# A decoder layer on one core: turned halves stored in two transfers instead of four, one load, eight weight casts and two additions moved

## The chip, the cores and the metric

The kernel runs on one core of a Trainium2 chip. The metric is the device time of one execution in microseconds (us). A core has a matrix engine (TensorE, PE in the rows; PEld are its weight loads), a vector engine (VectorE, DVE), an activation engine (ScalarE, ACT), a general engine (GpSimd, POOL) and a queue engine that issues transfers (SyncE, SP; SPq in the rows), besides 16 DMA engines that move the data. Each of the five runs its own list of instructions in order; they meet at semaphores, which count up when an instruction or a transfer is done.

## The reference, cut to what matters

```python
x = x + attn(layernorm(x))             # x: 2 x 512 x 1024, float32
x = x + fake_quant(layernorm(x)) @ fake_quant(ctx)   # ctx: 2 x 1024 x 1024
x = x + experts(layernorm(x))          # 64 experts of rank 8, top 16

def attn(h):                           # 32 query heads, 8 key/value heads of 128
    q, k, v = h @ Wq, h @ Wk, h @ Wv   # Wq 1024 x 4096, Wk and Wv 1024 x 1024
    q, k = rope(q), rope(k)            # second half of a head turned into the first
    p = softmax(causal(q @ k.T / sqrt(128)))
    return (p @ v) @ Wo                # Wo 4096 x 1024
```

Only the attention block is touched by the change.

## The kernel before, in words

Products in float32 are made of three passes: each factor is split into a high part (a rounded copy, type fp32r, by a cast) and a low part (factor minus high part), and hi·hi, hi·lo and lo·hi are summed in PSUM (`PASSES`). So each operand of PE costs one cast and one subtraction on other engines before PE can use it. The large products are made by a seven-product scheme of Winograd's kind (`P1` to `P7`) on quarters of the matrices.

After a first stage (four panels of Wq, Wk, Wv; some 160 us) the program runs 64 **units** `u`. A unit is one query head for one of the two batch rows. PE's list for a unit is: scores(u), one place of filling work, mix(u-1) (probabilities times values), a second place of filling work, and the transposes of the unit's probabilities (`turn_probs`, L1733), in three chunks. What fills:

- In units 1 to 56 it is **jobs**: 112 of them, `JOB_AT` says which at which unit and place. Seven jobs (`SEQ`: P1, P6, P2, P7, P5, P4, P3) make one **narrow panel** `e` of 16, that is two heads of q or k for both batch rows. VectorE reads each product (`read_job`); for P2/P4 (batch row 0) and P5/P3 (batch row 1) it multiplies with sine and cosine (L1293, L1294), GpSimd adds (`turn_added`) and SyncE stores the result to HBM (`keep_turned`, L556 to L563), once after P4 and once after P3. The tiles that hold the two **turned halves** `made_half(b, i)` lie in SBUF on 128 partitions: partitions 0 to 63 belong to head n = 0, partitions 64 to 127 to head n = 1; i = 0 holds the first half of the head's channels for n = 0 but the second for n = 1, and i = 1 the reverse. Each of the four pieces of 64 rows of 2 KB is one transfer of 128 KB. They count `q_kept[b]` up by 16 each, 64 for a panel and batch row.
- Three things wait for `q_kept`: VectorE before it overwrites the tiles for the next panel (P2 waits for row 0, L1326; P7 for row 1, L1322), SyncE before it loads a q or k of that panel (`load_q` L541, `load_kv` L531), and ScalarE once (`first_high`, f = 1, L1024).
- From unit 57 on it is **first steps** `f` = 0 to 15, two in a unit (`STEP_AT`): products of the heads' outputs with Wo. Step f needs a cast and a low part of `first_rows(f)` (ScalarE L1027, GpSimd L852) and a cast and a low part of a pair of weight rows w00, 128 x 1024 (`ob_hi`: ScalarE L1029; `ob_lo`: VectorE L1395, in `first_weight_low`). The rows are loaded by SyncE in `load_first(f)`, L600.

In units with an even number up to 56 VectorE also adds a block of PSUM to the previous unit's output (`add_pair`, L1387 to L1389), for which the second chunk of the transposes waits. In units 50, 52, 55 and 56 (`SHORT`) there is one job instead of two; in 50 and 52 (`HALVED`) PE runs half of that job, then mix, then the other half. After the units follow 48 larger steps of the output product and then the other two blocks, which the change doesn't touch.

Of the kernel before, what the change touches and what calls it, by code (L numbers as in the profile page):

```python
# [282 lines left out]
def attention(nc, held, es, x_t, Wq, Wk, Wv, Wo, cos_in, sin_in, quant_in, ctx_rows, qk_dram, v_dram, o_dram,  # L283
# [219 lines left out]
    def _(sp):  # L503
# [22 lines left out]
        def load_kv(h):  # L526
            g, b = h // 2, h % 2
            if h >= 1:
                sp.wait_ge(kv_lo, 2 * h)
            if g >= HPG:  # L530
                sp.wait_ge(q_kept[b], 64 * (panel_of("k", g) + 1))  # L531
            sp.dma_start(kv_raw[:, 0, :], qk_dram[g, b]).then_inc(kv_in, 16)
            sp.dma_start(kv_raw[:, 1, :].rearrange("p (j c) -> p j c", c=HEAD),
                         v_dram[b * H:(b + 1) * H, g * HEAD:(g + 1) * HEAD].rearrange("(j p) c -> p j c", p=P)
                         ).then_inc(kv_in, 16)

        def load_q(u):
            if u >= 2:
                sp.wait_ge(q_lo, u - 1)
            if u >= 8:  # L540
                sp.wait_ge(q_kept[batch_of(u)], 64 * (panel_of("q", 4 * (u // 8) + u % 4) + 1))  # L541
            sp.dma_start(q_raw[:, u % 2, :], qk_dram[GROUPS + 4 * (u // 8) + u % 4, batch_of(u)]
                         ).then_inc(q_in[u % 2], 16)

        def load_narrow(e):
# [3 lines left out]
            for k in range(2):  # L549
                sp.dma_start(nraw[:, e % 2, k].rearrange("p k a c -> p k (a c)"),  # L550
                             W[k * 512:k * 512 + 512, head * HEAD:(head + 2) * HEAD].rearrange("(k p) c -> p k c", p=P)
                             ).then_inc(n_in[e % 2][k], 16)

        def keep_turned(j):
            if SEQ[j % 7] not in TURNS:
# [3 lines left out]
            sp.wait_ge(turn_made, 2 * e + b + 1)  # L559
            for n, (x, y) in enumerate(((0, 1), (1, 0))):  # L560
                rows = slice(64 * n, 64 * n + 64)
                sp.dma_start(qk_dram[head + n, b, 64 * x:64 * x + 64], made_half(b, 0)[rows, :]).then_inc(q_kept[b], 16)
                sp.dma_start(qk_dram[head + n, b, 64 * y:64 * y + 64], made_half(b, 1)[rows, :]).then_inc(q_kept[b], 16)  # L563

# [101 lines left out]
        for u in range(1, UNITS):  # L666
# [4 lines left out]
            if u == LAST_JOB_UNIT:  # L671
                load_first(0)
            if (u - 1, 0) in JOB_AT:
                keep_turned(JOB_AT[u - 1, 0])
# [9 lines left out]
            if u == LAST_JOB_UNIT:  # L684
                for f in range(1, 4):
                    load_first(f)
            if 2 <= u <= LAST_JOB_UNIT + 1:
# [254 lines left out]
    def _(act):  # L942
# [75 lines left out]
        def first_high(f):  # L1018
# [4 lines left out]
            if f == 1:  # L1023
                act.wait_ge(q_kept[0], 64 * NARROW)  # L1024
            if f >= 2:
                act.wait_ge(first_done, f - 1)
            nc.scalar.copy(oa[0][:, f % 2, :, 0:256], first_rows(f)).then_inc(fa_hi, 1)  # L1027
            act.wait_ge(w00_in[q // 4], 64)
            nc.scalar.copy(ob[0][:, f % 2, :, :], w00[:, 2 * q:2 * q + 2, :]).then_inc(fb_hi, 1)  # L1029

# [154 lines left out]
    def _(dve):  # L1185
# [126 lines left out]
        def read_job(j, begun=False):  # L1312
# [7 lines left out]
            elif p == "P7":  # L1320
                if e:
                    dve.wait_ge(q_kept[1], 64 * e)  # L1322
                nc.vector.tensor_tensor(n_u[:, 1, :], b, n_p1[:], ALU.add).then_inc(job_read, 1)
            elif p == "P2":
                if e:
                    dve.wait_ge(q_kept[0], 64 * e)  # L1326
                job_turned(b, made_half(0, 1), made_half(0, 0))
# [64 lines left out]
        def first_weight_low(f):  # L1392
            q = f % PAIRS
            dve.wait_ge(fb_hi, f + 1)
            nc.vector.tensor_tensor(ob[1][:, f % 2, :, :], w00[:, 2 * q:2 * q + 2, :], as32(ob[0][:, f % 2, :, :]),  # L1395
# [157 lines left out]
        for u in range(UNITS):  # L1553
# [12 lines left out]
            if u in SHORT:  # L1566
                normalise(u)
            if (u - 1, 2) in JOB_AT:
                read_job(JOB_AT[u - 1, 2])
            elif (u - 1, 1) in JOB_AT:  # L1570
                read_job(JOB_AT[u - 1, 1], read_begun(u))
            if (u, 1) in STEP_AT and u != LAST_JOB_UNIT + 3:
# [3 lines left out]
            if u == LAST_JOB_UNIT:  # L1576
                begin_last(JOBS - 1)
            if 0 < u <= PAIRED and u % 2 == 0:
                add_pair(u - 1)
# [964 lines left out]
```

## Time and profile before

| what | value |
|---|---|
| median of 3 runs | 1269.94 us (1269.48 to 1271.03) |
| the profiled execution | 1270.15 us, its span 1268.4 us |
| PE busy | 1247.6 us, 98% of the span |
| VectorE, ScalarE, GpSimd busy | 851.1, 788.0 and 612.4 us |
| DMA engines busy, units 1 to 56 | 0.67 of the time of 16 |
| TensorE clock granted | full speed all the time |

All times in the rows are us from the start of the span; the 1.75 us between span and execution lie around it. PE idles for some 20 us in all. A wait of another engine matters only where PE waits behind it. "Share" of DMA is the mean over the 16 DMA engines; the view doesn't tell one of them from another.

### The profile page before, as it was taken

The page shows a single profiled execution, that of the slowest core. Times are in us where ns is not written, and L with a number is a line of the kernel's source. Part 1 is how long each engine was busy: PE and PEld are TensorE (multiplying, and loading weights), DVE is VectorE, ACT ScalarE, POOL GpSimd, SP SyncE. Part 2 cuts the span into 40 slices and gives each one's busy share as a digit, 9 for nine tenths or more (in the row PEclk, how much of TensorE's full clock was granted, in tenths as well). Part 3 has the DMA queues.
Part 4 walks back from the last instruction along what each step waited for, and adds up shares of the span by engine and source line. Part 5 has one row for each costly group of instructions (what it writes and reads, how often), then busy time and mean ns, then how long its engine had stood idle before and what let it go on. Part 6 is the DMA issues. An engine that isn't in the chain of part 4 may idle for free. (4 is left out here: it accounts for less than half of the span.)

```text
span 1268.4 us, 19734 instructions
## 1 busy us (share of the span) xinstructions
PE 1247.6 (98%) x6823; PEld 1073.4 (85%) x6831; DVE 851.1 (67%) x1919; ACT 788.0 (62%) x1601; POOL 612.4 (48%) x450
## 2 busy tenths in 40 slices
PE   9999999999999999999999999999999999999998
PEld 8898898888888888888888887878888888868787
DVE  7874735566666667666666666655786777988863
ACT  6412247677768777778777888873333367766530
POOL 4776766678767877778677756420000000021100
PEclk9999999999999999999999999999999999999999
DMA  8043154454857958649586588658864567401111
GB/s 282 18 137 130 59 158 157 146 172 134 245 154 205 243 175 233 175 109 232 151 225 183 113 249 287 211 171 260 295 191 127 164 212 256 147 3 34 50 43 50
DMA packets 122403, 208.72 MB, mean 165 GB/s; under 512 B 15409, under 2 KB 56369, under 8 KB 118721
## 3 DMA queue, kind: packets, MB, share of 16 engines
q1 hardware_dynamic: 118272, 178.10, 43.0%
q0 software_dynamic: 4032, 29.36, 12.2%
q8 instruction: 55, 0.90, 0.3%
q14 instruction: 44, 0.35, 0.1%
HBM read 147.40 MB, written 88.08 MB: 186 GB/s over the span
## 5 line engine op out<-in xcount | busy, mean ns | idle before, releaser
L1359 DVE TENSOR_TENSOR pT_lo<-banks,pT_hi 128x512 fp32r<-128x512 f32 (+1 forms) x192 | 103.6, 595 | 114.3 <-ACT pT_hi L1059 114.2
L1811 PE MATMUL banks<-ob_hi,oa_hi 128*128 128x512 f32 x384 | 149.4, 389 | 0.0
L1811 PE MATMUL banks<-ob_lo,oa_hi 128*128 128x512 f32 x384 | 149.4, 389 | 0.0
L1811 PE MATMUL banks<-ob_hi,oa_lo 128*128 128x512 f32 x384 | 149.4, 389 | 0.0
L1768 PE MATMUL banks<-xc,nring_hi_a 128*128 128x512 f32 x448 | 138.6, 390 | 0.7 <-DVE q_made L1294 0.3
L1768 PE MATMUL banks<-xc,nring_hi_b 128*128 128x512 f32 x448 | 138.6, 391 | 0.0
L1043 ACT CAST oa_hi<-oraw 128x1024 fp32r<-128x1024 f32 x48 | 50.4, 1050 | 127.0 <-PE banks L1811 114.8
L2031 POOL TENSOR_TENSOR resid<-resid,colterm 128x1024 f32<-128x1024 f32 x8 | 19.9, 2491 | 205.1 <-ACT colterm L2089 132.6
L1059 ACT CAST pT_hi<-banks 128x512 fp32r<-128x512 f32 (+1 forms) x192 | 86.6, 527 | 45.2 <-PE banks L1733 44.5
L1716 PE MATMUL banks<-kT,q_hi 128*128 128x512 f32 (+2 forms) x384 | 104.1, 352 | 0.0
L786 POOL TENSOR_TENSOR q_lo<-q_raw,q_hi 128x512 fp32r<-128x512 f32 x64 | 88.7, 1386 | 27.0 <-ACT q_hi L997 27.0
L1370 DVE CUSTOM_DVE_ANT_0 prob<-banks,mask 128x512 f32<-128x512 f32 (+2 forms) x192 | 101.1, 551 | 0.3 <-DVE resid L1265 0.3
L1406 DVE TENSOR_TENSOR oa_lo<-oraw,oa_hi 128x1024 fp32r<-128x1024 f32 x48 | 58.8, 1225 | 61.4 <-ACT oa_hi L1043 61.2
L1768 PEld LDWEIGHTS banks<-xc,nring_hi_a 128*128 128x128 f32 x448 | 80.4, 188 | 14.9 <-issue 1.7
L1768 PEld LDWEIGHTS banks<-xc,nring_hi_b 128*128 128x128 f32 x448 | 80.7, 188 | 13.7
L1066 ACT ACTIVATE banks<-prob,small 128x384 f32<-128x384 f32 (+2 forms) x192 | 89.3, 465 | 0.0
L791 POOL TENSOR_TENSOR nring_lo_a<-nraw,nring_hi_a 128x512 fp32r<-128x512 f32 x48 | 63.4, 1321 | 51.2 <-ACT nring_hi_a L1011 51.1
L1768 PE MATMUL banks<-xc,nring_lo_a 128*128 128x512 f32 x224 | 87.3, 390 | 0.0
L1768 PE MATMUL banks<-xc,nring_lo_b 128*128 128x512 f32 x224 | 87.3, 390 | 0.0
L1811 PEld LDWEIGHTS banks<-ob_hi,oa_hi 128*128 128x128 f32 x384 | 72.1, 188 | 15.1
L1811 PEld LDWEIGHTS banks<-ob_lo,oa_hi 128*128 128x128 f32 x384 | 72.1, 188 | 15.0
L1811 PEld LDWEIGHTS banks<-ob_hi,oa_lo 128*128 128x128 f32 x384 | 72.1, 188 | 14.8
(275 smaller groups left out, 3415.8 us busy)
## 6 DMA issues: line engine op xcount, KB each, us to landing
q_raw<-qk_dram SPq DMA_DIRECT2D x64, 256.0 KB, 3.8
o_S<-o_st SPq DMA_DIRECT2D x64, 256.0 KB, 3.1
w<-in_L_attn_Wo SPq DMA_DIRECT2D x32, 512.0 KB, 6.7
oraw<-o_S SPq DMA_DIRECT2D x32, 512.0 KB, 4.0
nraw<-in_L_attn_Wq SPq DMA_DIRECT2D x28, 512.0 KB, 6.0
o_S<-o_S POOLq DMA_DIRECT2D x12, 1024.0 KB, 10.1
o_S<-o_N POOLq DMA_DIRECT2D x12, 1024.0 KB, 10.7
resid<-in_x SPq DMA_DIRECT2D x16, 512.0 KB, 7.3
```

The lines of the kernel that those rows point to most:

```text
L786: nc.gpsimd.tensor_tensor(qh[1][:, u % 2, :], q_raw[:, u % 2, :], as32(qh[0][:, u % 2, :]), ALU.subtract).then_inc(q_lo, 1)
L791: nc.gpsimd.tensor_tensor(split(n_ring(1, j)), n_factor(j), split(as32(n_ring(0, j))), ALU.subtract).then_inc(n_lo, 1)
L1043: nc.scalar.copy(oa[0][:, s % 2, :, :], oraw[:, s % 2, :, :]).then_inc(oa_hi, 1)
L1059: nc.scalar.copy(pT[0][:, chunk_at(u, c):chunk_at(u, c) + CHUNK_WIDTH[c]], turned_chunk(turned, mixed, c)).then_inc(pT_hi, 1)
L1066: nc.scalar.activation(prob[:, sl] if n == 0 else score_tile(i), prob[:, sl], ACT.Exp, bias=shift[:, i:i + 1], scale=-1.0, accum_out=total ...
L1359: nc.vector.tensor_tensor(pT[1][:, sl], turned_chunk(turned, mixed, c), as32(pT[0][:, sl]), ALU.subtract).then_inc(pT_lo, 1)
L1370: nc.vector.tensor_tensor_reduce(out=prob[:, PROB_AT[i]:PROB_AT[i] + w], in0=score[:, s, c:c + w], in1=mask[:, H - w:H] if i else first_ma ...
L1406: nc.vector.tensor_tensor(oa[1][:, s % 2, :, :], oraw[:, s % 2, :, :], as32(oa[0][:, s % 2, :, :]), ALU.subtract).then_inc(oa_lo, 1)
L1716: ins = nc.tensor.matmul(score[:, s, c:c + w], qh[a][:, u % 2, i * P:(i + 1) * P], kT[e][:, h % 2, 0:w], start=(p == 0), stop=(p == 2))
L1768: ins = nc.tensor.matmul(job_bank(j), n_ring(a, j)[:, k * P:(k + 1) * P], xc[:, XI[p], c, k, :], start=(opens and k == 0 and n == 0), stop ...
L1811: ins = nc.tensor.matmul(step_bank(m, t), oa[a][:, s % 2, k, t * P:(t + 1) * P], ob[c][:, s % 2, k, :], start=(q == 0 and k == 0 and i == ...
L2031: nc.gpsimd.tensor_tensor(resid[:, t, :], resid[:, t, :], colterm[:, t // TPB, :], ALU.add).then_inc(col_added, 1)
```

## The change

1. `keep_turned` stores each SBUF tile of 128 partitions in one transfer of 256 KB. The target in HBM is then a list of two pieces of 64 rows that are five (or three) pieces apart. `q_kept` counts to 32 for a panel and batch row instead of 64, and the four places that wait for it follow.
2. In unit 56 SyncE issues `load_first(1)` together with `load_first(0)`, ahead of the stores of that unit, and no longer behind them.
3. For even first steps (f = 0, 2, ..., 14) VectorE makes the cast of the weight pair itself, right ahead of its subtraction; ScalarE makes it for odd f only.
4. In units 50 and 52 VectorE's `add_pair` comes before `read_job`; in unit 52 the first addition of that job (`begin_last`) is taken ahead of it.

```diff
-                sp.wait_ge(q_kept[b], 64 * (panel_of("k", g) + 1))
+                sp.wait_ge(q_kept[b], 32 * (panel_of("k", g) + 1))
...
+        qk_halves = qk_dram.rearrange("h b (x r) c -> (h b x) r c", r=64)
+
         def keep_turned(j):
...
-            for n, (x, y) in enumerate(((0, 1), (1, 0))):
-                rows = slice(64 * n, 64 * n + 64)
-                sp.dma_start(qk_dram[head + n, b, 64 * x:64 * x + 64], made_half(b, 0)[rows, :]).then_inc(q_kept[b], 16)
-                sp.dma_start(qk_dram[head + n, b, 64 * y:64 * y + 64], made_half(b, 1)[rows, :]).then_inc(q_kept[b], 16)
+            first = 4 * head + 2 * b
+            for i, halves in enumerate((slice(first, first + 6, 5), slice(first + 1, first + 5, 3))):
+                sp.dma_start(qk_halves[halves], made_half(b, i)).then_inc(q_kept[b], 16)
...
             if u == LAST_JOB_UNIT:
                 load_first(0)
+                load_first(1)
...
             if u == LAST_JOB_UNIT:
-                for f in range(1, 4):
-                    load_first(f)
+                load_first(2)
+                load_first(3)
...
             nc.scalar.copy(oa[0][:, f % 2, :, 0:256], first_rows(f)).then_inc(fa_hi, 1)
-            act.wait_ge(w00_in[q // 4], 64)
-            nc.scalar.copy(ob[0][:, f % 2, :, :], w00[:, 2 * q:2 * q + 2, :]).then_inc(fb_hi, 1)
+            if f % 2:
+                act.wait_ge(w00_in[q // 4], 64)
+                nc.scalar.copy(ob[0][:, f % 2, :, :], w00[:, 2 * q:2 * q + 2, :]).then_inc(fb_hi, 1)
...
         def first_weight_low(f):
             q = f % PAIRS
-            dve.wait_ge(fb_hi, f + 1)
+            if f % 2:
+                dve.wait_ge(fb_hi, f // 2 + 1)
+            else:
+                if f:
+                    dve.wait_ge(first_done, f - 1)
+                else:
+                    dve.wait_ge(job_done, JOBS)
+                dve.wait_ge(w00_in[q // 4], 64)
+                link(nc.vector.tensor_copy(ob[0][:, f % 2, :, :], w00[:, 2 * q:2 * q + 2, :]))
...
+            third = u in HALVED and SEQ[JOB_AT[u - 1, 1] % 7] == "P3"
+            if third:
+                begin_last(JOB_AT[u - 1, 1])
+            if u in HALVED:
+                add_pair(u - 1)
...
-                read_job(JOB_AT[u - 1, 1], read_begun(u))
+                read_job(JOB_AT[u - 1, 1], read_begun(u) or third)
...
-            if 0 < u <= PAIRED and u % 2 == 0:
+            if 0 < u <= PAIRED and u % 2 == 0 and u not in HALVED:
                 add_pair(u - 1)
```

On SyncE, in unit 56 of the program before: `oraw` are the rows of the first steps, `n_turn` the turned halves of batch row 0, `n_sin` and `n_u` those of row 1.

```order
L600 DMA oraw<-o_A 128x2x256
L562 DMA qk_dram<-n_turn 64x512
L563 DMA qk_dram<-n_turn 64x512
L562 DMA qk_dram<-n_turn 64x512
L563 DMA qk_dram<-n_turn 64x512
L542 DMA q_raw<-qk_dram 128x512 x2
L600 DMA oraw<-o_A 128x2x256 x3
```

The same place of the program after:

```order
L602 DMA oraw<-o_A 128x2x256 x2
L565 DMA qk_dram<-n_turn 2x64x512 x2
L542 DMA q_raw<-qk_dram 128x512 x2
L602 DMA oraw<-o_A 128x2x256 x2
L572 DMA o_N<-o_st 128x512
L576 DMA w<-in_L_attn_Wo 128x2x512 x2
L565 DMA qk_dram<-n_sin 2x64x512
L565 DMA qk_dram<-n_u 2x64x512
```

The second load of rows stands ahead of the stores, and a store's target is written with an outermost count of 2. All other transfers on SyncE keep their shape.

On VectorE, in unit 52 before (`banks` is PSUM, `late` and `o_st` belong to `add_pair`, `q_made` to the read of P3):

```order
L1382 RECIPROCAL small<-small 128x3
L1310 TENSOR_TENSOR banks<-banks,n_u 128x512
L1293 TENSOR_TENSOR q_made<-banks,sin 128x512
L1294 TENSOR_TENSOR q_made<-banks,cos 128x512
L1387 COPY late<-banks 128x128
L1388 TENSOR_TENSOR banks<-banks,late 128x128
L1389 TENSOR_TENSOR o_st<-o_st,banks 128x128
```

and after:

```order
L1386 RECIPROCAL small<-small 128x3
L1314 TENSOR_TENSOR banks<-banks,n_u 128x512
L1391 COPY late<-banks 128x128
L1392 TENSOR_TENSOR banks<-banks,late 128x128
L1393 TENSOR_TENSOR o_st<-o_st,banks 128x128
L1297 TENSOR_TENSOR q_made<-banks,sin 128x512
L1298 TENSOR_TENSOR q_made<-banks,cos 128x512
```

`add_pair` moved ahead of two multiplications.

## Rows read from the trace of the kernel before

**Rows 1.** The page, parts 1 and 3: busy us (share); queue: packets, MB, share
```profile
PE 1247.6 (98%) x6823; PEld 1073.4 (85%) x6831; DVE 851.1 (67%) x1919; ACT 788.0 (62%) x1601; POOL 612.4 (48%) x450
...
q1 hardware_dynamic: 118272, 178.10, 43.0%
```

**Rows 2.** Busy us by stretch: length, PE, PEld, DVE, ACT, POOL, clock, DMA share, GB/s
```profile
200.00:760.00 560.00, 557.91 (x3038) 486.43 (x3037) 362.70 (x1066) 430.88 (x1078) 413.38 (x336) 1.00 0.67 184
760.00:850.00 90.00, 84.05 (x452) 71.63 (x451) 55.45 (x127) 73.69 (x162) 43.00 (x29) 1.00 0.69 221
850.00:1060.00 210.00, 210.00 (x928) 173.89 (x927) 150.62 (x133) 94.83 (x96) 4.91 (x6) 1.00 0.69 216
```

**Rows 3.** Waits of PE from 700 to 850 us: total, times, longest
```profile
PE banks L1785 <- DVE ob_lo L1395: 3.8, 6, 1.3
...
PE banks L1785 <- issue: 0.7, 1, 0.7
PE banks L1733 <- DVE o_st L1389: 0.6, 1, 0.6
```

**Rows 4.** Timeline of PE: start, us, line, operation [idle before, and its releaser]
```profile
724.97 1.11 PE L1733 MATMUL banks<-ident,prob 128*128 128x128 f32 x6 [0.63 <-DVE o_st L1389]
...
771.37 0.47 PE L1785 MATMUL banks<-ob_hi,oa_hi 128*128 128x512 f32 x1 [1.20 <-DVE ob_lo L1395]
...
841.93 0.47 PE L1785 MATMUL banks<-ob_hi,oa_hi 128*128 128x512 f32 x1 [1.29 <-DVE ob_lo L1395]
```

**Rows 5.** Timeline of VectorE in units 52 and 60
```profile
724.11 0.28 DVE L1387 COPY late<-banks 128x128 f32<-128x128 f32 x1
...
807.88 1.29 DVE L1401 COPY p<-banks 128x512 f32<-128x512 f32 x2 [3.03 <-PE banks L1785]
809.09 1.22 DVE L1395 TENSOR_TENSOR ob_lo<-w,ob_hi 128x1024 fp32r<-128x1024 f32 x1
```

**Rows 6.** Timeline of ScalarE in unit 57
```profile
765.04 0.62 ACT L997 CAST q_hi<-q_raw 128x512 fp32r<-128x512 f32 x1
768.15 0.62 ACT L1027 CAST oa_hi<-oraw 128x512 fp32r<-128x512 f32 x1 [2.49 <-DMA oraw<-o_A]
```

**Rows 7.** Groups by line and shape on VectorE: busy us, mean ns, idle before
```profile
L1474 DVE TENSOR_SCALAR raw<-raw 128x1024 f32<-128x1024 f32 x16 | 11.1, 694 | 7.2 <-ACT raw L1092 7.2
...
L1420 DVE TENSOR_TENSOR w<-w 128x1024 f32<-128x1024 f32 x8 | 9.8, 1219 | 0.0
```

**Rows 8.** Timeline of SyncE's queue: first store of a pair, loads behind
```profile
230.25 0.59 SPq L562 DMA_DIRECT2D qk_dram<-n_turn  x1
...
234.66 0.45 SPq L562 DMA_DIRECT2D qk_dram<-n_sin  x1
...
728.01 0.45 SPq L562 DMA_DIRECT2D qk_dram<-n_sin  x1
...
757.68 0.45 SPq L562 DMA_DIRECT2D qk_dram<-n_turn  x1
...
762.34 0.82 SPq L542 DMA_DIRECT2D q_raw<-qk_dram  x2
```

**Rows 9.** Transfers by kind: times, KB each, median us from issue to landing
```profile
q_raw<-qk_dram SPq DMA_DIRECT2D x64, 256.0 KB, 3.8
...
qk_dram<-n_turn SPq DMA_DIRECT2D x64, 128.0 KB, 2.7
...
out<-resid SPq DMA_DIRECT2D x7, 512.0 KB, 2.6
...
out<-resid SPq DMA_DIRECT2D x2, 256.0 KB, 2.0
```

**Rows 10.** Timeline of VectorE: the read of P7, first and last panel
```profile
245.76 0.69 DVE L1323 TENSOR_TENSOR n_u<-banks,n_p 128x512 f32<-128x512 f32 x1 [0.86 <-PE banks L1768]
...
743.35 0.69 DVE L1323 TENSOR_TENSOR n_u<-banks,n_p 128x512 f32<-128x512 f32 x1
```

**Rows 11.** Waits of the whole span, the longest of VectorE: total, times, longest
```profile
DVE pT_lo L1359 <- ACT pT_hi L1059: 114.2, 49, 4.5
```

More of the change, by code:

```diff
@@ L540, in load_q @@
             if u >= 8:
-                sp.wait_ge(q_kept[batch_of(u)], 64 * (panel_of("q", 4 * (u // 8) + u % 4) + 1))
+                sp.wait_ge(q_kept[batch_of(u)], 32 * (panel_of("q", 4 * (u // 8) + u % 4) + 1))
             sp.dma_start(q_raw[:, u % 2, :], qk_dram[GROUPS + 4 * (u // 8) + u % 4, batch_of(u)]
@@ L1023, in first_high @@
             if f == 1:
-                act.wait_ge(q_kept[0], 64 * NARROW)
+                act.wait_ge(q_kept[0], 32 * NARROW)
             if f >= 2:
@@ L1321, in read_job @@
                 if e:
-                    dve.wait_ge(q_kept[1], 64 * e)
+                    dve.wait_ge(q_kept[1], 32 * e)
                 nc.vector.tensor_tensor(n_u[:, 1, :], b, n_p1[:], ALU.add).then_inc(job_read, 1)
@@ L1325, in read_job @@
                 if e:
-                    dve.wait_ge(q_kept[0], 64 * e)
+                    dve.wait_ge(q_kept[0], 32 * e)
                 job_turned(b, made_half(0, 1), made_half(0, 0))
```

## The prediction

> **What bounds the kernel now.** I read the busy times first: PE is busy 98% of the span [rows 1], at full clock throughout [rows 2]. By stretch it idles 2.1 us in the 560 us of the jobs, 6.0 us in the 90 us of the last jobs and the first steps, and not at all in the 210 us behind them [rows 2]. So all that this change can win lies in those 8 us. The waits of PE name the part it aims at: 3.8 us for the low parts of the weights, 0.7 us that no releaser explains at the first step, 0.6 us for `add_pair` [rows 3]. In the timeline three of them stand out: 0.63 us in unit 52, 1.20 us before step 1, 1.29 us before step 14 [rows 4]. The other side of the account is the DMA engines. They are off PE's path today, but busy 0.67 of the time of all 16 during the jobs [rows 2]; whatever narrows that has some 560 us in which to hurt.
>
> **Part by part: the three edits on the engines.**
>
> *`add_pair` earlier (unit 52).* PE waits 0.63 us [rows 4] for additions that begin at 724.11 [rows 5]. They move ahead of two multiplications of about 0.6 us each from start to start, so they end 1.2 us sooner and the wait goes: -0.6. What is late next is GpSimd's turned half, which has over 5 us to its store's use. In unit 50 PE doesn't wait today: 0.
>
> *`load_first(1)` earlier.* ScalarE idled 2.49 us for these rows before the cast at 768.15 [rows 6], and the whole chain behind it (cast of rows, cast of weights, low part, step 1) ended in PE's 1.20 us [rows 4]. Loaded ahead of the stores the rows are there at 760, and the cast can follow q_hi at 765.7. VectorE reaches the low part after its score work 1.1 us before it did. So -1.2, if nothing else in that place gets late. ScalarE's cast also waits for `q_kept[0]`, which comes from the stores, and the q_hi just ahead of it reads a q that was stored only five us before [rows 6, 8]. This is where edit 1 can take it back.
>
> *The even casts.* ScalarE loses 8 casts, VectorE gains 8. No row shows this cast on VectorE; the nearest with one source and the same 128x1024 in SBUF is 694 ns, the nearest with two is 1219 ns [rows 7]. Not below 694, since nothing of its size is shorter. I take 0.7, by the row with one source. In most units it is hidden: VectorE idles 3 to 4 us there, where it waited for ScalarE. Two places are exposed. Before step 8 VectorE first copies two banks and then makes the low part, back to back [rows 5]; PE reaches the step as this ends, so the cast adds 0.5 us there (1.0 with 1219 ns). Before step 15 the low part stands behind the transposes' low parts; step 14 gets rid of its 1.29 us but 0.7 of it returns as a longer wait for step 15. The other waits for `ob_lo` (3.8 less 1.2 and 1.3) go, since ScalarE's pT_hi comes 0.5 us sooner. With slower restarts of PE saved, some 0.8 us over ten places: -1.3 + 0.7 + 0.5 - 1.3 - 0.8 - 0.3 at the first step = -2.5, or -2.0 with the slow cast.
>
> Sum of the three: -0.6 - 1.2 - 2.5 = -4.3; with -5.5 and -3 as ends.
>
> **The stores.** SyncE issues 64 transfers fewer, 0.6 us each [rows 8]; it is no bound, so that is worth 0. The price lies in the shape. Every transfer of the kernel before has the same outermost count on both sides, 128, 64 or 16, all multiples of 16. The new ones have 128 partitions on one side and an outermost count of 2 on the other. No row shows how such a transfer is cut for the 16 engines. The ends:
>
> - Spread over 16: 256 KB land like the q loads, 3.8 us, where 128 KB took 2.7 [rows 9]. Price 0.
> - Cut by what both outermost counts share, which is 2: 128 KB for each of two engines. An engine's rate comes from two rows: 256 KB more in `out` took 0.6 us more, 16 KB an engine, 27 GB/s [rows 9]; over all of q1, 178.1 MB in 0.43 of 16 x 1268 us is 20.4 GB/s [rows 1]. So a transfer holds its two engines 4.8 to 6.4 us, and a landing has 1.4 us on top (2.0 less 0.6).
>
> I take the second, since a cut that gives 16 engines equal shares has to divide a row of pieces that is only two long; the nearest row (128 on both sides) is of another kind. The Trainium skill says so outright (DMA: Bandwidth & Descriptors, "Why a DMA increments its semaphore by 16 and not by 1"): the number of engines is the largest up to 16 that divides the slowest dimension of both access patterns. It is a rule against this change. No run here shows it yet; by it the sum is the one below, without it the first rival's.
>
> What that costs. A panel has two pairs of stores, the second on average 5.5 us behind the first (4.4 in the first panel) [rows 8], and everything SyncE issues queues behind them on these two engines. The second pair lands 1.4 + 4 x (4.8 to 6.4) + 0.7 (a q load in between) - 5.5 = 15.8 to 22.2 us after its issue. VectorE reads P7 of the next panel, which waits for that, 11.1 us after it in the first case and 15.3 in the last, 13.5 on the mean of 15 [rows 8, 10]. So VectorE comes 2.3 to 8.7 us late per panel, 5.5 in the middle. The loads of keys, values and q issued behind the pair are late by the same. VectorE has some cover, 2.3 us of idle before each pT_lo (114.2 in 49) [rows 11]; it isn't all at the right place, as GpSimd's accumulating transfers share the engines too. I count half: 4.3 x 15 = 65 us. At the low end cover takes all: 0; at the high end none: 130.
>
> Twice a q is loaded right behind its own store: for unit 50 and for unit 58. For 58 the pair is issued at 757.7 and q_hi ran at 765.0 [rows 6, 8]. Now the pair lands at 757.7 + 1.4 + 9.6 to 12.8 and the load 3.8 later: 772.5 to 775.7, late by 7.5 to 10.7, and ScalarE stands still meanwhile. Step 1's 1.2 us are lost with it, within the unit's other lateness. Say 8 for each, 16 in all.
>
> Sum: 1270.15 - 4.3 + 65 + 16 = 1346.9; the profiled execution is 0.2 above the median, which changes nothing. **Forecast 1347.**
>
> **Rivals.**
>
> 1. *The stores are spread over 16 engines after all.* Then they cost nothing, a pair even lands a little sooner, and only the three edits are left: 1270 - 4.3 = 1265.5, from 1264.5 to 1267. For it speaks that the source side has 128 partitions, which alone would do. This is the other side of zero. It decides at the store's landing: under 4 us it holds. Chance 0.12.
> 2. *Two engines, but the cover is larger than I think.* The pair's lateness falls where VectorE waits for ScalarE anyway, with the fast rate: only the two tight loads stay, 2 x 6: 1270 - 4.3 + 12 = 1278. Against it: in the first panels the read of P7 stands ahead of the reciprocals that the transposes need, so it delays PE directly. It lies inside the slow case's range.
> 3. *Two engines, and they become the bound.* Their share would be 0.67 x 35 us = 23 us of a panel's 35, less 2.7 that their stores take today, plus 19 to 26: 40 to 47 us. If that queue never drains, each panel lasts 5 to 12 us longer: 16 x 12 - 4 = 190 more, 1455 at worst, 1346 at best. Against the upper part: packets of different queues overlap on an engine. Chance 0.06 for over 1425.
> 4. *Spread over 16, but the casts on VectorE cost more* (1219 ns and held up by GpSimd's subtractions, from 1.5 us a cast on): steps 8 and 15 take 2 us back, 1268 to 1270. Chance 0.03.
>
> **How the numbers follow.** Two engines: 0.85 in all (of it 0.79 between 1277 and 1425, 0.06 above). Spread over 16: 0.12 plus 0.03. Range of the forecast: low 1270 - 4.3 + 0 + 12 = 1278, high 1270 - 4.3 + 130 + 21 = 1417, 8 more for GpSimd's transfers: 1277 to 1425. It holds 0.79. Faster by over 0.2% (2.5 us, about what a measurement can tell from no change) needs a spread over 16 with the edits as worked out: 0.12. Within 0.2%: 0.03 for rival 4, nothing more. Slower: 0.85.
>
> **What the profile after would show.** Right: the landing of `qk_dram<-n_turn` goes from 2.7 to 10 us or more, that of q loads from 3.8 up; new rows in which VectorE's L1327 (the read of P7) and ScalarE's q_hi and kT wait for DMA; PE idle between 200 and 760 goes from 2 us to some 70, at the transposes and scores; GB/s falls while the share of all 16 engines doesn't rise. The three edits: no wait of PE on `add_pair` in unit 52, no 1.2 us before step 1 unless q_hi is late, 0.5 us before step 8. Wrong: stores landing in under 4 us, the job stretch within 1 us of 560, and 1265. If the stores land late but PE doesn't idle, the cover was mis-sized, not the spread.

## The result, and the profile after

The changed kernel takes **1443.97 us** (median of 4 runs, 1440.76 to 1445.2) where the kernel before took 1270.49 beside it (4 runs, 1269.48 to 1272.13): ratio 1.136, 95% interval 1.1347 to 1.1374. It is 174 us slower; 77 were predicted, and the range ended at 1425. The profiled execution has a span of 1439.0 us in a run of 1440.8.

From the page of the changed kernel, the lines that answer to [rows 1]: span, busy times, granted clock in 40 slices, and the hardware queue with its packets, MB and share of 16 engines:

```profile
span 1439.0 us, 19686 instructions
PE 1289.4 (90%) x6831; PEld 1102.0 (77%) x6831; DVE 858.9 (60%) x1927; ACT 779.0 (54%) x1593; POOL 607.3 (42%) x450
PEclk9999999999898899999799898989999999999999
q1 hardware_dynamic: 116352, 178.10, 37.0%
```

The span grew by 170.6. PE's idle time is span less busy time: 20.8 us before, 149.6 now, so 129 us of it; the other 42 are PE's own busy time, 1247.6 before and 1289.4 now, for the same work at a lower clock. The MB are the same to the last digit. The packets are 1920 fewer. That number names the cut: if a transfer leaves one closing packet with each engine that it uses, the 128 old stores with 16 engines each had 2048, and 64 new ones with 2 engines have 128; the difference is 1920. The records of the single packets in the trace say the same more directly: exactly two packets are in flight during 230.4 us of the changed kernel, and during 17.8 us of the one before.

The windows answer to [rows 2] (length, busy time of the five engines, granted clock, DMA share, GB/s):

```profile
200.00:760.00 560.00, 468.09 (x2371) 401.83 (x2370) 282.68 (x821) 331.99 (x831) 327.18 (x265) 0.91 0.50 143
200.00:930.00 730.00, 605.68 (x3088) 520.46 (x3086) 374.71 (x1087) 432.60 (x1086) 418.67 (x339) 0.92 0.50 142
1020.00:1230.00 210.00, 210.00 (x930) 173.93 (x929) 150.08 (x133) 94.31 (x95) 4.91 (x6) 1.00 0.69 215
```

The stage of the jobs now runs from 200 to about 930 instead of 760: 730 us for 16 panels, 45.6 each, 11 more than the 35 of before. In the 90 us behind it (930 to 1020, the last jobs and the first steps) PE idles 13.3 us in place of 6.0. Behind that nothing changed: the last row is PE without idle time, as in [rows 2] at 850 to 1060. The mean of all 16 DMA engines *fell* from 0.67 to 0.50. Two overloaded engines don't show in a mean of 16.

PE's waits, us in total, times, longest (the first rows, against [rows 3]), then who waits for DMA:

```profile
PE banks L1750 <- ACT o_st L1091: 74.5, 13, 15.6
PE banks L1785 <- DVE n_u L1327: 23.5, 7, 7.0
PE banks L1750 <- ACT prob L1082: 16.5, 12, 5.5
...
PE banks L1785 <- DVE n_turn L1298: 10.9, 4, 5.0
```

```profile
ACT q_hi L1000 <- DMA q_raw<-qk_dram: 97.0, 16, 9.8
DVE n_u L1327 <- DMA qk_dram<-n_u: 93.7, 13, 17.2
...
ACT o_st L1091 <- DMA o_S<-o_st: 49.1, 9, 11.1
...
DVE n_turn L1297 <- DMA qk_dram<-n_turn: 27.4, 6, 7.7
```

Three kinds of buffers are late: the panels' (n_u, n_turn), q, and the one of the attention's output, o_st. The largest wait of PE comes by the third, which the prediction doesn't name. The landing of a q load (64 loads, KB each, median us), against the 3.8 of [rows 9]:

```profile
q_raw<-qk_dram SPq DMA_DIRECT2D x64, 256.0 KB, 8.7
```

SyncE's DMA issues in the first turned panel, start and duration, against the 0.5 to 0.6 us of one issue in [rows 8], and VectorE's two reads that wait for these stores:

```profile
230.60 1.43 SPq L565 DMA_DIRECT2D qk_dram<-n_turn  x2
232.07 4.15 SPq L542 DMA_DIRECT2D q_raw<-qk_dram  x1
236.26 0.54 SPq L565 DMA_DIRECT2D qk_dram<-n_sin  x1
236.84 4.85 SPq L565 DMA_DIRECT2D qk_dram<-n_u  x1
241.74 3.42 SPq L532 DMA_DIRECT2D kv_raw<-qk_dram  x1
245.20 2.73 SPq L533 DMA_DIRECT2D kv_raw<-v_dram  x1
247.97 2.51 SPq L572 DMA_DIRECT2D o_A<-o_st  x1
250.53 1.88 SPq L572 DMA_DIRECT2D o_S<-o_st  x3
```

```profile
244.67 0.69 DVE L1297 TENSOR_TENSOR n_turn<-banks,sin 128x512 f32<-128x512 f32 x1 [7.67 <-DMA qk_dram<-n_turn]
255.58 0.69 DVE L1327 TENSOR_TENSOR n_u<-banks,n_p 128x512 f32<-128x512 f32 x1 [6.12 <-DMA qk_dram<-n_u]
```

The first pair is through 14.1 us after its issue at 230.6, the second 19.3 after 236.3. In 13 panels VectorE's read of P7 waits for the second pair; it starts 13.3 to 29.5 us after that pair's issue, 19.3 at the median. And an issue itself is now long: SyncE stands still inside the issue behind these stores, and whatever comes next in its order is held, the output stores too. The longest issue is that of an output store, 15.3 us, where the longest of an output store was 2.3 before; it precedes PE's longest wait:

```profile
688.36 15.33 SPq L572 DMA_DIRECT2D o_N<-o_st  x1
```

```profile
713.72 0.69 PE L1750 MATMUL banks<-ident,prob 128*128 128x128 f32 x2 [15.62 <-ACT o_st L1091]
```

The steps from one to the other show later in the stage, SyncE's queue, PE's last short wait, then ScalarE and PE:

```profile
866.55 1.03 SPq L565 DMA_DIRECT2D qk_dram<-n_turn  x2
867.80 7.09 SPq L542 DMA_DIRECT2D q_raw<-qk_dram  x1
874.98 0.91 SPq L572 DMA_DIRECT2D o_A<-o_st  x1
```

```profile
870.03 0.44 PE L1750 MATMUL banks<-ident,prob 128*128 128x128 f32 x2 [0.70 <-ACT o_st L1091]
...
```

```profile
890.57 0.60 ACT L1091 ACTIVATE o_st<-banks 128x512 f32<-128x512 f32 x1 [12.77 <-DMA o_A<-o_st]
891.22 0.69 PE L1750 MATMUL banks<-ident,prob 128*128 128x128 f32 x2 [11.01 <-ACT o_st L1091]
```

The output store is issued 7 us late (the last addition to its buffer ends at 868.2) and lands 15.6 us after that; ScalarE waits 12.77 us to write the buffer again, PE 11.01 us for ScalarE. The two matmuls then take 0.69 us; after the short wait at 870.03 two of them took 0.44. PE comes back at the lower of its two clock levels: the granted clock between 889.5 and 893 us is 0.50, where it was 1.00 between 866 and 879.

### The profile page after: what moved, and what is told of

It reads as the page before. It is cut to its first block and busy times, and to the rows that moved or that the text cites. A ratio compares the mean times of both kernels' runs of the same rounds, so it can differ in the third digit from the quotient of the medians.

```text
span 1439.0 us, 19686 instructions
## 1 busy us (share of the span) xinstructions
PE 1289.4 (90%) x6831; PEld 1102.0 (77%) x6831; DVE 858.9 (60%) x1927; ACT 779.0 (54%) x1593; POOL 607.3 (42%) x450
## 2 busy tenths in 40 slices
DMA packets 120482, 208.71 MB, mean 145 GB/s; under 512 B 13488, under 2 KB 54448, under 8 KB 116800
## 3 DMA queue, kind: packets, MB, share of 16 engines
q1 hardware_dynamic: 116352, 178.10, 37.0%
q0 software_dynamic: 4032, 29.36, 10.9%
## 5 line engine op out<-in xcount | busy, mean ns | idle before, releaser
L1750 PE MATMUL banks<-ident,prob 128*128 128x128 f32 x640 | 87.6, 282 | 91.0 <-ACT o_st L1091 74.5
L1785 PE MATMUL banks<-xc,nring_hi_a 128*128 128x512 f32 x448 | 146.2, 409 | 18.4 <-DVE n_u L1327 14.5
L1785 PE MATMUL banks<-xc,nring_hi_b 128*128 128x512 f32 x448 | 143.1, 401 | 16.1 <-DVE n_u L1327 8.9
L1750 PEld LDWEIGHTS banks<-ident,prob 128*128 128x128 f32 x640 | 74.2, 144 | 106.3 <-ACT o_st L1091 77.8
L1828 PE MATMUL banks<-ob_hi,oa_hi 128*128 128x512 f32 x384 | 149.6, 390 | 0.0
L789 POOL TENSOR_TENSOR q_lo<-q_raw,q_hi 128x512 fp32r<-128x512 f32 x64 | 87.7, 1371 | 81.3 <-ACT q_hi L1000 81.3
L1733 PE MATMUL banks<-kT,q_hi 128*128 128x512 f32 (+2 forms) x384 | 114.1, 381 | 0.0
L1785 PEld LDWEIGHTS banks<-xc,nring_hi_a 128*128 128x128 f32 x448 | 85.4, 200 | 34.6 <-issue 19.9
L794 POOL TENSOR_TENSOR nring_lo_b<-nraw,nring_hi_b 128x512 fp32r<-128x512 f32 x48 | 63.3, 1320 | 99.8 <-ACT nring_hi_b L1014 99.8
L1091 ACT ACTIVATE o_st<-banks 128x512 f32<-128x512 f32 x64 | 38.3, 598 | 106.8 <-DMA o_S<-o_st 49.1
L1000 ACT CAST q_hi<-q_raw 128x512 fp32r<-128x512 f32 x64 | 41.0, 640 | 97.0 <-DMA q_raw<-qk_dram 97.0
L1785 PE MATMUL banks<-xc,nring_lo_a 128*128 128x512 f32 x224 | 91.0, 406 | 0.0
```

The lines of the kernel that those rows point to most:

```text
L789: nc.gpsimd.tensor_tensor(qh[1][:, u % 2, :], q_raw[:, u % 2, :], as32(qh[0][:, u % 2, :]), ALU.subtract).then_inc(q_lo, 1)
L794: nc.gpsimd.tensor_tensor(split(n_ring(1, j)), n_factor(j), split(as32(n_ring(0, j))), ALU.subtract).then_inc(n_lo, 1)
L1733: ins = nc.tensor.matmul(score[:, s, c:c + w], qh[a][:, u % 2, i * P:(i + 1) * P], kT[e][:, h % 2, 0:w], start=(p == 0), stop=(p == 2))
L1750: ins = nc.tensor.transpose(dst[:, col:col + P], prob[:, PROB_AT[i] + j * P:PROB_AT[i] + (j + 1) * P], ident[:])
L1785: ins = nc.tensor.matmul(job_bank(j), n_ring(a, j)[:, k * P:(k + 1) * P], xc[:, XI[p], c, k, :], start=(opens and k == 0 and n == 0), stop ...
L1828: ins = nc.tensor.matmul(step_bank(m, t), oa[a][:, s % 2, k, t * P:(t + 1) * P], ob[c][:, s % 2, k, :], start=(q == 0 and k == 0 and i == ...
```

## The experiments

Eighteen kernels ran. "Scratch" means a kernel whose turned rows go to a tensor of their own that nobody reads, so that only shape and timing of the stores are in play. All ratios are to the kernel before on the same chip.

**Which edit, and is it the shape?** `stores2x64` has the store edit alone; `plain128` differs from it in the target only:

```
-            for i, halves in enumerate((slice(first, first + 6, 5), slice(first + 1, first + 5, 3))):
-                sp.dma_start(qk_halves[halves], made_half(b, i)).then_inc(q_kept[b], 16)
+            for i in range(2):
+                sp.dma_start(qk_dram[head + i, b], made_half(b, i)).then_inc(q_kept[b], 16)
```

> The kernel before with the store edit alone (two transfers of 2 x 64 rows per turned pair in place of four of 64 rows); the other three edits are left out. Theory A, the stores carry the whole loss and the other edits give about 4 us where they act: 1443.97 + 4.3 = about 1448 us, 1443 to 1452. Rival B, the loss needs the other edits too (add_pair or the casts falling behind the late panels on VectorE): at least 10 us under 1444, so below 1434. The q1 hardware queue should show the 116352 packets of the changed kernel, not the 118272 of before.

> As the kernel with the store edit alone, with one thing changed: each of the two transfers goes to one plain panel of 128 rows of the same tensor instead of to two runs of 64 rows with a distance between them. Bytes, source tile, number of transfers, waits and places in SyncE's order are the same; the rows of the two heads of a pair are exchanged in part, so the attention is computed on mixed heads. Theory A, the outermost count of 2 at the destination confines each transfer to two DMA engines: here the outermost count is 128, so the time returns to that of before or a little under it (1270.5, 1266 to 1272) and a q load lands in 3.8 us again. Rival B, it is the size or the number of the transfers (256 KB from 128 partitions in one issue, two counts of 16 in place of four): the time stays at about 1448 us.

Measured: `stores2x64` 1445.65 us, ratio 1.1382 (1.1366 to 1.1398); `plain128` 1269.72 us, 0.9994 (0.9985 to 1.0003). Theory A holds in both. The same bytes from the same 128 partitions in the same 64 transfers cost nothing if the target's outermost count is 128. Rival B of each is out. The saved issues are worth nothing, as predicted.

**The dose.** The scratch kernels cut the target of each transfer into 2, 4, 8 or 16 pieces. This is the store with 2 pieces; with 4, 8 and 16 the last range is 0:32, 0:16 and 0:8:

```
+                sp.dma_start(t_dram[e, b, i, :, 0:64], made_half(b, i)).then_inc(q_kept[b], 16)
```

> The kernel before with the turned panels stored by two transfers of 256 KB per pair into a scratch tensor, whose destination is 2 pieces of 64 rows with a gap behind each; the four heads of the second stage on read the panels of the first stage again instead of the turned ones, so the attention of the later heads is computed on other data. Counts, waits and places in the order are those of the store edit. Control of the form: Theory A, the time depends on the destination's outermost count alone, so this is as slow as the store edit, about 1445 us (1435 to 1455). Rival B, the distance between the pieces or the tensor that is written sets the cost: elsewhere, below 1400.

> As the scratch kernel with 2 pieces, with 4 pieces of 32 rows in the same transfers. Theory A, the transfer is cut over as many DMA engines as its outermost count allows: four engines with 64 KB each, half the time of two (half of 13 to 22 us late), 1285 to 1340 us, and 4 completion packets per transfer: 64 packets more in the queue than with 2 pieces. Rival B, any cut destination costs the same: about 1445 us.

> As before with 8 pieces of 16 rows. Theory A: eight engines, a store lands within some 6 us, hidden by the panel's own cover: 1268 to 1280 us. Rival B: about 1445 us.

> As before with 16 pieces of 8 rows. Theory A: all 16 engines, 1266 to 1272 us, the kernel before in all but the number of issues. Rival B: about 1445 us.

Measured: 1445.77, 1300.34, 1273.86 and 1269.93 us; ratios 1.1371 (1.1338 to 1.1404), 1.0228 (1.0181 to 1.0274), 1.0032 (1.0011 to 1.0053) and 0.9994 (0.9983 to 1.0005). The hardware queue's row of the pages, in the same order:

```profile
q1 hardware_dynamic: 116352, 178.10, 37.0%
q1 hardware_dynamic: 116480, 178.10, 41.3%
q1 hardware_dynamic: 116736, 178.10, 42.2%
q1 hardware_dynamic: 117248, 178.10, 42.1%
```

128, 384 and 896 packets more than with 2 pieces are 64 transfers x 2, 6 and 14: each transfer uses as many engines as it has pieces (the expectation said 64 more for 4 pieces, a slip of mine: there are 64 transfers, not 32). The packet records agree: exactly four packets are in flight during 84.1 us of the kernel with 4 pieces (9.1 before), exactly eight during 46.7 us of the one with 8 (12.6 before). Doubling the engines cuts the loss from 175 to 30 us, then to 3 or 4. So the loss isn't proportional to the time of a store: it falls faster than the bytes on each engine, and with eight engines nearly all is hidden. Here is also the Trainium skill's rule (DMA: Bandwidth & Descriptors, "Why a DMA increments its semaphore by 16 and not by 1"), the largest number up to 16 that divides the slowest dimension of both sides: 2, 4, 8 and 16 engines for these counts against 128 partitions. The packets agree with it in each case.

**Number of engines, or the time that they need?** `one2` leaves out the second of the two transfers (`range(1)`, waits adapted), with 2 pieces.

> The scratch kernel with 2 pieces and only the first of the two transfers of each pair; the second half of the turned rows is not stored. The two engines then carry as many bytes each as in the kernel with 4 pieces (64 KB twice there, 128 KB once here), which took 1300 us. Theory E, the time that the busiest engines need sets the loss: 1290 to 1320 us. Theory F, it is the number of engines, or every transfer picks its own pair of engines so that the second never queued behind the first: above 1380 us.

Measured: 1297.52 us, 1.0209 (1.0125 to 1.0293), as with 4 pieces. Theory E: two engines with 128 KB each cost what four with twice 64 KB cost. And leaving out the second transfer takes away 148 of 175 us, which speaks for its standing behind the first on the same engines. So do the packet records: with 2 pieces and both transfers exactly four packets are in flight for only 17.1 us, exactly two for 234.1; `one2` has two in flight for 100.9 us.

**Which wait carries it? The output stores.** `outs_act` takes them out of SyncE's order:

```
+            if 0 < u < UNITS - 1:
+                act.wait_ge(o_copied, u)
+                for name in o_names(u - 1):
+                    nc.scalar.dma_start(o_dram[name][o_place(u - 1)[1]], o_st[(u - 1) % 2][:]
+                                        ).then_inc(o_kept[(u - 1) % 2], 16)
```

> The changed kernel with one thing more: the stores of the attention's output (o_st) are issued by ScalarE, on its own queue, one unit after they are made, and not by SyncE behind the turned halves; the last two stay with SyncE. Nothing is left out of the computation. In the changed kernel TensorE waits 74.5 us for o_st (line 1750), which waits for the output stores, and SyncE's own issues take up to 9 us behind the two-engine stores. Theory A, the output stores held back in SyncE's order are the path: o_st's waits for the DMA go, and 50 to 75 us with them, with some of the 42 us that the lower clock adds: 1350 to 1395 us. Rival B, the time is bound by the turned rows' own arrival (VectorE's wait at line 1327 and ScalarE's for q_raw), and TensorE's idle time only moves to those rows: 1425 to 1445 us.

> Control: the kernel before with the same move of the output stores to ScalarE's queue. ScalarE has 62 % busy and gives some 100 issues of under 0.1 us each: 1270 to 1278 us, by every theory. What it is over 1270.5 is the price of the move itself.

Measured: 1462.21 us, ratio 1.1511 (1.1496 to 1.1527), the control 1285.87 us, 1.0123 (1.0109 to 1.0137). Both expectations missed. The control is 15.6 us over the kernel before, where 0 to 8 were expected: a store's issue takes ScalarE's own time, at least 0.33 us and not under 0.1. In the control ScalarE sat idle 48.0 us in 34 places ahead of its copies to o_st, with nothing but its own issues there. Take these 16 off, and `outs_act` stands at 1446 to 1447, a little over the 1444 of the change. That takes the price of the move to be the same in both kernels, which no run shows; but nothing of the 50 to 75 us of theory A is to be seen. PE's waits in `outs_act`:

```profile
PE banks L1788 <- DVE n_u L1330: 81.3, 14, 12.8
PE banks L1788 <- DVE n_turn L1301: 24.2, 8, 5.8
PE banks L1753 <- ACT prob L1080: 17.4, 9, 5.3
...
PE banks L1753 <- ACT o_st L1094: 6.3, 8, 2.1
```

The 74.5 us for o_st are gone, all but 6.3, and 81.3 + 24.2 for the panels stand in their place, where 23.5 + 10.9 stood before. Theory A, my reading of the largest row of the waits, fell. What the run takes away is the output stores' place in SyncE's order; they still share the two engines.

**The panels' buffers, and q.** Scratch kernels with 2 pieces. `still2` lets the stores read a table that nobody rewrites, so VectorE's wait for them can go (SyncE waits in its place for the stores of the panel before, which have landed by then); `noq2` leaves out the q loads of the later units; `still_noq2` does both:

```
-                sp.dma_start(t_dram[e, b, i, :, 0:64], made_half(b, i)).then_inc(q_kept[b], 16)
+                sp.dma_start(t_dram[e, b, i, :, 0:64], (cos, sin)[i][:] if e < NARROW - 1 else made_half(b, i)).then_inc(q_kept[b], 16)
...
-                    dve.wait_ge(q_kept[1], 32 * e)
+                    dve.wait_ge(turn_made, 2 * e)
```

```
         def load_q(u):
+            if u >= 8:
+                return
```

> The scratch kernel with 2 pieces (1445.8 us), in which the stores of the first 15 turned pairs of each batch read the tables of cosines and sines, which nobody writes in this stage, in place of the turned halves. VectorE therefore need not wait for the stores to land before it writes the next panel. The turned rows are thus not stored, and later heads read the first stage's as in that kernel. Places, bytes and the cut over two engines are unchanged. Theory P, VectorE's wait for its buffers is the loss: 1270 to 1330 us. Theory Q, the loads of q behind the stores are the loss: 1420 to 1446 us. Both in one, each enough by itself: in between, 1350 to 1420 us, with ScalarE's wait for q_raw as the largest.

> The scratch kernel with 2 pieces, without the loads of q from unit 8 on: ScalarE splits what the first eight loads left, so the scores are those of other heads. VectorE's wait for its buffers stays. Theory P: 1400 to 1446 us. Theory Q: 1270 to 1330 us. Both in one: in between, with VectorE's wait at line 1323 as the largest.

> Both edits: stores that read the tables, and no loads of q from unit 8 on. All three theories: under 1300 us, unless the output stores held in SyncE's order or the loads of k and v behind the same engines carry a part by themselves; what is over 1270 is that part.

Measured: 1441.0 us (1.1338, 1.1305 to 1.1371), 1415.13 (1.1135, 1.1102 to 1.1167) and 1402.92 (1.1039, 1.1007 to 1.1071). So 5, 31 and 43 of the 175 us come back. `still2` came out as theory Q has it, `noq2` as theory P: neither wait is the loss alone, and both together aren't either, since 132 us are left in `still_noq2`. The expectation had named what they would then be, the output stores or the loads of k and v. PE's waits in it, the two first rows, and what ScalarE waited for:

```profile
PE banks L1739 <- ACT o_st L1093: 97.1, 12, 18.7
PE banks L1791 <- DVE ob_lo L1401: 8.3, 6, 4.8
```

```profile
ACT o_st L1093 <- DMA o_S<-o_st: 87.9, 10, 15.0
```

Now nearly all of PE's added waits stand at the output stores, whose place in SyncE's order `outs_act` had shown to be worth nothing alone. I read the four runs together as substitutes: three kinds of transfer stand behind the turned stores, and PE waits for whichever is left. This isn't shown to the end. All three taken away at once wasn't tried, nor the turned stores issued by another engine, which would part the hold in SyncE's order from the load of the two engines. And `noq2` leaves out 256 KB a unit too, so its 31 us may be less traffic as well as one wait less.

**Are the two engines full?** The last pair adds traffic that nobody waits for to the changed kernel and to the one before:

```
+            if 8 <= u < 52:
+                sp.dma_start(x_dram[u], qk_dram[GROUPS + u % 4, 0]).then_inc(x_kept, 16)
```

> The changed kernel with 44 more transfers of 256 KB, one in each unit from 8 to 51, from one place in HBM to another, that nobody reads; nothing is left out of the computation. Each puts 8 packets of 2 KB on every engine, 84 to 95 ns each by the packets of this trace, 0.7 to 0.8 us. Theory B, the two engines are the bound of the stage: 44 x 0.7 to 0.8 = 31 to 34 us more, 1475 to 1478; the 45 q loads of this stage that the kernel without them saved gave 31 us, which is 0.68 each. Theory L, the loss is a chain of late landings of the turned rows and the q loads alone: the added transfers stand ahead of a few of them, under 12 us more, 1444 to 1456.

> Control: the same 44 transfers added to the kernel before. By both theories they are hidden there, since each engine is busy 0.67 of this stage and would be busy 0.73: 1270 to 1275 us.

Measured: 1454.47 us, 1.1453 (1.1411 to 1.1495), which is 10.5 over the changed kernel, or 11.8 by the ratios, with some 6 to 17 us as interval; the control 1271.32, 1.0007 (0.9996 to 1.0018). Theory L wanted under 12, so it isn't told apart from somewhat more; theory B's 31 to 34 are out. The expectation had the transfers' shape wrong: the queue has 1408 packets more, 32 for each transfer, 16 of them closing ones, so each engine moves one packet of 16 KB and not 8 of 2 KB. The control's queue is busy 45.0% of its span against 43.0%, which is 27 us more on each engine. So the added work costs nothing in the kernel before and something between a quarter and two thirds of its engine time here. By an estimate the two engines are nearly full, if all other traffic is spread evenly: of the stage's 0.50 x 730 = 365 us for each engine some 320 aren't turned stores, and these put 64 x 4.8 to 6.4 = 307 to 410 us on each of the two, in all 86 to 100% of 730. But they aren't an unbroken bound, since 27 us of added work would then cost 27, and in the changed kernel no packet at all is in flight during 86 to 91 of the stage's 730 us. That leaves the two engines at most 88% busy: full in bursts, with slack between.

**The three small edits.** `edits234` undoes the store edit; `casts` and `load1` have one edit each (hunks of the change shown above, alone); `edits234_early8` is `edits234` with one more call moved:

```
+            if (u + 1, 0) in STEP_AT:
+                first_weight_low(STEP_AT[u + 1, 0])
             if (u, 1) in STEP_AT and STEP_AT[u, 1] == PAIRS - 1:
                 keep_first_pass()
-            if (u + 1, 0) in STEP_AT:
-                first_weight_low(STEP_AT[u + 1, 0])
```

> The changed kernel with the store edit undone (four transfers of 64 rows per pair again): the earlier load of the second first-pass block, the even casts of the first pass on VectorE, and the earlier add of a pair remain. Theory A, the three edits are worth what the prediction worked out, -0.6 -1.2 -2.5 = -4.3 us: ratio 0.9966, about 1266.2 us. Rival B, VectorE is bound in the first pass and the copies of 0.7 us each come back in full (7 even casts in steps, about 5 us): ratio 1.000 to 1.001. Rival C, only the loads matter: ratio 0.999.

> The three edits without the store edit, and one more: in the unit that computes step 7 of the first pass, VectorE makes the weights of step 8 ahead of reading step 7's banks instead of behind it. Theory: step 8's wait of TensorE for the weights (0.5 us in the prediction) goes, so 0.3 to 0.6 us under the kernel with the three edits alone (ratio to it 0.9995 to 0.9998, at the edge of what can be told). Rival: the reading of step 7's banks is what the next product waits for, and the order costs 0.5 to 1.5 us instead.

> The kernel before with the even casts of the first pass on VectorE alone. The three edits together gave 0.9985 (0.9975 to 0.9994), not the 0.9966 that the prediction had. Theory A, the casts give what the prediction said, 2.5 us, and the loads and the add less: ratio 0.9980. Theory B, the copy of 0.7 us on VectorE, which stands just ahead of the weights that TensorE waits for, takes most of it back: ratio 0.9995 to 1.0005, and the 0.7 us wait of the first step of the pass grows to 1.1 us as in the trace of the three edits.

> The kernel before with the second block of the first pass loaded one place earlier, alone. Theory A, as predicted: the 1.20 us wait of TensorE at the second step goes, ratio 0.9991. Theory B, that wait ends on VectorE's cast, not on the load, so the load alone changes nothing: ratio 1.0000, the wait of 1.2 us stands. The two are 1.2 us apart, at the edge of what the times can tell; the trace tells it.

Measured: `edits234` 1268.42 us, 0.9985 (0.9975 to 0.9994); `edits234_early8` 1265.87, 0.9967 (0.9956 to 0.9979); `casts` 1268.97, 0.9988 (0.9979 to 0.9996); `load1` 1268.62, 0.9988 (0.9979 to 0.9997). Of the theories for `edits234` only C, 0.999, lies in the interval. For `casts` both 0.9980 and 0.9995 do, so its time decides nothing; the trace has to. `load1` is theory A. PE's waits between 724 and 850 us, first in `edits234` and then in `casts`, against [rows 3]:

```profile
PE banks L1801 <- issue: 2.5, 2, 1.3
PE banks L1801 <- DVE ob_lo L1406: 1.1, 1, 1.1
PE banks L1749 <- ACT prob L1081: 0.9, 2, 0.7
```

```profile
PE banks L1794 <- issue: 2.3, 2, 1.2
PE banks L1794 <- DVE ob_lo L1404: 1.1, 1, 1.1
```

and the three places in the timeline of `casts` where PE idles for a first-pass step (0, 8 and 15):

```profile
765.92 0.47 PE L1794 MATMUL banks<-ob_hi,oa_hi 128*128 128x512 f32 x1 [1.12 <-issue]
...
808.90 0.47 PE L1794 MATMUL banks<-ob_hi,oa_hi 128*128 128x512 f32 x1 [1.20 <-issue]
...
842.21 0.47 PE L1794 MATMUL banks<-ob_hi,oa_hi 128*128 128x512 f32 x1 [1.10 <-DVE ob_lo L1404]
```

The 1.20 us ahead of step 1 [rows 4] are gone in `casts` and in `load1` too: each edit alone removes that wait, so it counts once. Step 14's 1.29 us are gone in `casts` too, and step 15 waits 1.10 in place of 0.27 us, 0.8 more where 0.7 were predicted. The casts cost 0.4 at step 0 (0.74 before) and 1.2 at step 8. With the 0.6 for `add_pair` the trace gives 4.5 us of waits in this window in place of 6.5: -2.0, as the ratio has it (-1.9). In `edits234_early8` step 8's wait is gone, but 0.91 and 0.76 us stand elsewhere, and the waits in the window sum to 4.8. Its time is 2.5 us under `edits234`, with intervals that overlap; its trace shows no gain. It is the fastest kernel of the study, by 0.3% under the one before; whether the moved call has part in that stays open.

## Why the prediction was wrong

**Right: the direction, the culprit, the cut.** The store edit is the whole loss (`stores2x64`), because of the outermost count and nothing else (`plain128`), and two engines carry each transfer (packets, dose, `one2`). Rivals 1 and 4, spread over 16, are out.

**Right: the landing.** 15.8 to 22.2 us were worked out for the second pair; 19.3 was measured in the first panel and as the median of 13, though 5 of the 13 lie over the range, up to 29.5. The q loads rose from 3.8 to 8.7.

**Wrong: the step "What that costs", the cover.** It priced one consumer, VectorE's read of P7, at 5.5 us late, and took off half of 2.3 us of cover: 4.3 a panel, 65 in all. Measured is 11 us a panel; between 200 and 760 us PE idles 92 us, where some 70 were forecast. Three things are in that difference.

- *The other consumers.* The step notes that loads of q, keys and values "are late by the same", and prices them at nothing beyond two tight places (16 us). ScalarE waited for q in 16 places, 97 us in all. The output stores aren't in it at all, though they stand behind the turned ones in the same order. PE idles 129 us more. `still2` shows that even without VectorE's wait 170 of the 175 us stay. So the priced term is neither the loss nor a part that could be added to others: the 65 stood for a wait that is worth 5 when it is removed alone.
- *SyncE's issue.* The queue was thought of as one that takes every issue in 0.6 us. It took up to 15.3, and held the next transfers of an order with three late buffers in it. How much of the loss that is, apart from the landing, no run separates.
- *The clock.* PE's busy time is 41.8 us longer, at a granted clock of 0.91 to 0.92 in the stage, that is partly at the lower of its two levels, 1.2 in place of 2.4 GHz. It fell only where PE idled: with 4 pieces and little idle time it was 0.99, and PE busy 1253.5 us. The prediction has no such term. Idle and clock together, 129 + 42, are the span's 171, but as an account, not as two causes: at full clock PE might have idled longer in the same waits.

**Rival 3 came nearest.** It had 5 to 12 us more a panel, 1346 to 1455, with a chance of 0.06 above 1425; the panel got 11 longer. (Its upper end is 1270 + 16 x 12 - 4 = 1458, not 1455.) Its argument against itself, that packets of different queues overlap, has little to bear on here: the turned stores and nearly all that waits behind them are issued by SyncE, on one queue (116352 of the page's 120482 packets). What spoke for it was that two engines at 40 to 47 us of work in a panel of 35 leave no cover for anybody. Its picture of a queue that never drains isn't borne out in full (`extra2`). That its sum contains the measured time is in part luck: it has no term for the clock either.

**The three edits**: -4.3 predicted, -1.9 measured (0.9985, interval -3.2 to -0.8). Wait for `add_pair`: right. The second load: right by itself (`load1`, -1.5), but the casts remove the same 1.2 us. Step 8: 0.5 predicted, 1.2 measured. So the mis-sized term is the casts', -2.5, which are -1.5 alone by the median (interval -2.7 to -0.5), and with the load the two gains overlap. Within it steps 14 and 15 came as predicted; step 8 took back 0.7 us more, step 0 got 0.4 worse where 0.3 were to be gained, and the 0.8 us for slower restarts show in no row.

## What to carry to other kernels

Before two transfers are merged into one, look at the outermost count that is left on each side: it sets over how many DMA engines the bytes go. Here two engines cost 175 us, four 30 and eight 3 or 4, although the bytes were the same. Price such a change by what the busiest engine then carries in one period against the period's length, not by one waiting read. When a queue in program order gets slow, look at everything that stands behind it. Here the largest wait in the profile was only the first in line, and removing it showed the next.

## What the hardware showed that I had not expected

- An issue on SyncE isn't free of what stands on the DMA engines: 0.5 us for the first transfer of a pair, 4.3 at the median and up to 9.1 for the last (n_u). With 4 pieces the median of the last was 0.58 and the longest 4.4, with 8 it never passed 0.92, though single output stores still took up to 6.1 us to issue there. The two rows are of the line of the stores, with 2 pieces and with 4 (ns, min/median/max):

```profile
L563 SPq DMA_DIRECT2D t_dram<-n_u x16: 506/4324/8929, 236.5 to 938.2; - x16
```

```profile
L563 SPq DMA_DIRECT2D t_dram<-n_u x16: 511/577/4446, 235.5 to 794.3; - x16
```

- Three output stores in a row hold ScalarE for 2.56 us when ScalarE issues them, in the control that has no slow store. 110 such issues cost that kernel 16 us:

```profile
230.94 2.56 ACTq L1086 DMA_DIRECT2D o_S<-o_st  x3
```

- Packets overlap on a DMA engine: in the kernel before more than 16 are in flight, on 16 engines, during 233 us by the times of their records, at most 27 at once.
- One transfer of 256 KB over all 16 engines in each of 44 units, added to a kernel whose engines were busy 0.67 of the stage, was free (1.0007).
